# Last token group: indirect stores of units 5 to 8 on GpSimd behind four added waits on TensorE semaphores

## The reference

```python
xn = _layernorm(x)
# L1 attention: r, k, v are products with xn; a cumulative sum over time; a norm per batch; a product with Wo
r = sigmoid(xn @ Wr.T); k = xn @ Wk.T; v = xn @ Wv.T
state = cumsum(k * v / scale, axis=time) * scale
normed = groupnorm(r * state) * gn_weight + gn_bias
attn = normed @ Wo.T
# L1 mixture: the two best experts of each token, softmax weights
top_w, top_i = top_k(xn @ gate_w.T, 2)
ffn = sum over the two experts of softmax(top_w) * (xn @ expert_w[e] + expert_b[e])
x = x + attn + ffn
```

## Time and profile before

| | us |
|---|---|
| device time, median of 3 runs | 438.25 (437.61 to 438.61) |
| device time of the profiled execution | 437.0 |
| its span in the profile | 435.3 |
| PE busy in the span | 418.9 |
| DVE busy | 345.7 |
| ACT busy | 183.6 |
| POOL busy | 170.7 |
| chain that ended last: share of PE, DVE, issue, POOL | 78%, 11%, 3%, 2% |

### The profile page before, as it was taken

How to read it: one execution, slowest core, us unless ns; L and a number is a source line. 1 busy time by engine, 2 the same in 40 slices (tenths; PEclk the granted TensorE clock), 3 DMA queues, 4 the chain that set the end, 5 groups by cost and what they waited for, 6 DMA issues and landing times.

```text
span 435.3 us, 7440 instructions
## 1 busy us (share of the span) xinstructions
PE 418.9 (96%) x2488; PEld 364.5 (84%) x2488; DVE 345.7 (79%) x1087; ACT 183.6 (42%) x361; POOL 170.7 (39%) x200
## 2 busy tenths in 40 slices
PE   7999999999999999999999999999999999889992
PEld 5788888978898989788899898788999898779882
DVE  6799998898997677989968788899795757268781
ACT  4745654442364456332734343336352342423130
POOL 1556469621054104310447325103420445606456
PEclk9999999999999999999999999999999999999997
DMA  8992899950011310000112200000107545302289
GB/s 278 399 321 81 232 268 271 271 149 2 0 58 40 98 49 2 0 1 2 49 49 69 78 2 1 2 0 31 68 2 203 186 121 164 105 12 75 75 215 279
DMA packets 30373, 46.87 MB, mean 108 GB/s; under 512 B 2696, under 2 KB 24480, under 8 KB 29824
## 3 DMA queue, kind: packets, MB, share of 16 engines
q1 hardware_dynamic: 25984, 35.75, 27.5%
q0 software_dynamic: 3360, 9.85, 7.8%
q10 hardware_dynamic: 992, 0.81, 0.6%
HBM read 22.74 MB, written 23.65 MB: 107 GB/s over the span
## 4 chain that ended last, share of the span: by engine, by line
PE 78%; DVE 11%; issue 3%; POOL 2%; another core or an unknown queue 2%; ACT 2%; DMA 1%; POOLq 0%; DVEq 0%; ACTq 0%
PE D L707 23%; PE G L707 21%; PE U L707 20%; PE M L707 7%; PE D L738 1%; DVE mid_lo L1366 1%; DVE mid L1489 1%; DVE rows L1503 1%; POOL sums_gate L656 1%; DVE carry_gain L1727 1%; PE M L857 1%; DMA rows<-x 1%; PE M L832 1%; DVE gamma L1729 1%
## 5 line engine op out<-in xcount | busy, mean ns | idle before, releaser
L707 PE MATMUL D<-w_hi,mid_hi 128*128 128x256 f32 x260 | 74.1, 285 | 0.1
L707 PE MATMUL D<-w_hi,mid_lo 128*128 128x256 f32 x260 | 73.6, 283 | 0.0
L707 PE MATMUL D<-w_lo,mid_hi 128*128 128x256 f32 x260 | 73.5, 283 | 0.0
L1108 ACT ACTIVATE mid<-G 128x512 f32<-128x512 f32 x64 | 37.8, 594 | 72.3 <-PE G L707 46.4
L1489 DVE TENSOR_TENSOR mid<-mid,U 128x512 f32<-128x512 f32 x64 | 42.7, 683 | 21.8 <-ACT mid L1108 10.5
L551 POOL TENSOR_TENSOR w_lo<-w_raw,w_hi 128x512 fp32r<-128x512 f32 x35 | 50.3, 1469 | 22.9 <-ACT w_hi L1077 12.1
L1503 DVE SCALAR_TENSOR_TENSOR rows<-D,weight,rows 128x256 f32<-128x256 f32 x128 | 54.0, 476 | 6.4 <-PE D L707 3.9
L1077 ACT ACTIVATE mid_hi<-mid 128x512 fp32r<-128x512 f32 x64 | 39.8, 631 | 38.6 <-DVE mid L1489 37.0
L1366 DVE TENSOR_TENSOR mid_lo<-mid,mid_hi 128x512 fp32r<-128x512 f32 x64 | 49.7, 797 | 4.8 <-ACT mid_hi L1077 3.3
L707 PEld LDWEIGHTS D<-w_hi,mid_hi 128*128 128x128 f32 x260 | 49.8, 191 | 1.8 <-issue 1.1
L707 PE MATMUL G<-xT_hi,w_hi 128*128 128x512 f32 x126 | 50.4, 400 | 0.3 <-POOL w_lo L551 0.3
(11 more groups left out here) (369 smaller groups left out, 956.0 us busy)
## 6 DMA issues: line engine op xcount, KB each, us to landing
sorted_rows<-weighted SPq DMA_DIRECT2D x8, 1542.0 KB, 20.1
stage<-sorted_rows SPq DMA_DIRECT2D x31, 128.5 KB, 2.1
w_raw<-weights SPq DMA_DIRECT2D x2, 1280.0 KB, 14.3
w_raw<-weights SPq DMA_DIRECT2D x2, 1024.0 KB, 22.9
rows<-x SPq DMA_DIRECT2D x7, 256.0 KB, 3.0
w_raw<-weights SPq DMA_DIRECT2D x2, 768.0 KB, 8.8
part<-rows SPq DMA_DIRECT2D x12, 128.0 KB, 2.3
sums_gate<-part SPq DMA_DIRECT2D x3, 512.0 KB, 7.2
```

The source lines that it names most:

```text
L707: ins = nc.tensor.matmul(out_ap, a, b, start=(first and n == 0), stop=(last and n == 3 * len(pairs) - 1))
L1108: nc.scalar.activation(mid[:, c, :], GU[2 * c][:, :], ACT.Silu).then_inc(silu_ready, 1)
```

## The change

In the last part of POOL's program, `return_rows(u)` gets one more wait for u = 5, 6, 7 and 8, after the two that it has and ahead of the unit's two indirect DMAs:

```diff
@@ -640,6 +640,10 @@
                 tiles = UNIT_TILES[u]
                 pool.wait_ge(to_row_made, u + 1)
                 pool.wait_ge(unit_evicted, u + 1)
+                if u == 5:
+                    pool.wait_ge(unit_ps, 8)
+                elif u in (6, 7, 8):
+                    pool.wait_ge(rkv_ps, at(LAST, 6, 2 * (u - 6) + 1))
                 for i, n in enumerate(tiles):
                     nc.gpsimd.indirect_dma_start(returned[:, :], bass.IndirectOffsetOnAxis(to_row[:, n:n + 1], 0),
                                                  made[u][:, i, :], None).then_inc(made_stored, 16)
```

## The result

| | before | after |
|---|---|---|
| median of the runs beside each other (us) | 437.93 (437.08 to 438.61, 4 runs) | 433.13 (432.57 to 433.61, 4 runs) |
| the profiled execution (us) | 437.0 | 432.89 |
| its span (us) | 435.3 | 431.2 |

The ratio is 0.9887, 95% interval 0.9871 to 0.9903: faster by 1.1%, or 4.8 us, where 3.0 were forecast. Here and in the experiments, ratios and ranges leave out two disturbed executions, one of the kernel before at 687 us and one of the last experiment's kernel at 1259 us.

The account below looks back on a forecast made before the run. PE, 78% of the chain, was taken as held by late increments under POOL's scatters. Gains 0.8 + 1.4 + 0.6 + 0.6 = 3.4 us, taken as 3.0, made 437.0 into 434.0, plus 1.25: 435.3 (8 in 10: 432.9 to 438.3).

Parts of the forecast that it names:

- The reading of the lag: At 379 to 383 us: TensorE's increments are handed on late, 2.5 to 5.4 us, while POOL has been scattering for a while.
- Step 1: Router in the last group: the logits' copy runs at 375.9, so PE's transpose L744 doesn't wait; 0.81 us.
- Step 2: PE behind that transpose: r of half 1, due at 381.5, no longer starts at 382.87; 1.4 us.
- Step 3: DVE's chain from `den_e` starts earlier, so unit 9's product on PE no longer waits until 388.26; 0.6 us.
- Step 4: PE's idle of 0.52 us ahead of unit 10's product, the same DVE queue one step later, goes; 0.6 us.
- 2.8 to 3.4 of shift for the last scatter: POOL's last scatter, at 412.71, on which the kernel's end hangs, comes 2.8 to 3.4 us earlier; taken as 3.0.
- More: Rival, chance 0.10: later scatters shift so that a delay among units 10 to 12 goes; 2 us more, 433.3.
- The four waits cost nothing.: POOL's waits for units 5 to 8 are free while unit 9's eviction is later than unit 8's pair.
- Partly: Rival, chance 0.17: a pair after a pause of 0.8 to 1.6 us still delays something; gain 0.8 to 1.8, 437.0.
- Slower: Rival, chance 0.12: any pair's second scatter delays, and pairs now lie over critical PE results; 1.2 us lost, 439.5.
- No change: Rival, chance 0.11: the stop at 379 to 383 us has another cause, or the tail's DMAs set the end; 438.2.
- Code loading: Possible other cause of the stop, within a rival of chance 0.11: one instruction block moved between 370 and 383 us.

Follow-up runs that it names:

- the last experiment's kernel: The changed kernel with one wait more, unit 4's pair also waiting for unit 7's product: median 431.71 us, ratio 0.9910 to the kernel before.
- the short fill: Kernel before with one GpSimd fill of 128x256 ahead of each pair of units 5 to 8, no waits: 436.55 us, ratio 0.9970.
- the first kernel with unit 4's put apart: Against the change, unit 4's pair waits too (unit 7's product) and units 5 to 8 wait one product later: 433.93 us, ratio 0.9917 to before.
- The long pause: Kernel before with three GpSimd fills of 128x512 ahead of each pair of units 5 to 8, no waits: 429.69 us, ratio 0.9996.

## Why the prediction was right, by its own steps

- **The reading of the lag.** `den_e`, `r_half` and the logits' copy were held by TensorE's late increments, and these by the run of scatters. Shown: moving the run moved the hold (to 386 to 404 us), splitting it in two left 2.1 us of PE's stops where another sitting's trace of before has 3.8, and with four pairs and unit 4's put apart as well none was left. That it is TensorE's increments and not every engine's, one hand-over inside the run shows: ACT's copy of the logits ends at 379.52 and PE, waiting for it, starts at 379.57. What the prediction did not see is the condition: on two other chips twelve scatters in a row hold nothing back. The trace of before could not tell this.
- **Step 1, the logits' copy, 0.8.** It starts at 376.21 (forecast 375.9), and PE reaches its transpose at 378.89 instead of 379.57: 0.7. (The trace of after runs 0.26 us late before the change begins, 356.88 against 356.62 for unit 1's first scatter, so each lead here is 0.26 too small.)
- **Step 2, 1.4.** r of half 1 starts at 380.79 instead of 382.87: 2.1 ahead, 1.4 more.
- **Step 3, 0.6.** Unit 9's product starts at 385.54 instead of 388.26: 2.7 ahead, 0.6 more.
- **Step 4, 0.6.** Unit 10's starts at 387.41 (forecast 387.4) instead of 390.91: 3.5 ahead, 0.8 more.
- **The last scatter, where the sum was too small.** The term "2.8 to 3.4 of shift for the last scatter", taken as 3.0, measured 4.0. From unit 9's first scatter to the last POOL took 21.36 us before (391.35 to 412.71) and takes 20.07 after (388.61 to 408.68): units 9 to 15 take 1.3 us less (18.71 on the second chip, where nothing is late). One late copy accounts for as much: unit 13's product came out 1.9 us late before (402.37, then 404.30) and 0.7 after (398.86, then 399.51). The prediction had named this as what it could place to 1.5 us at best. Which of them lose less can't be read in advance from the trace of before. SP's fetch of the returned rows (L514) waits for the same landings as the join, which the part on the kernel before leaves out; so the end hangs on the last scatter by both ways.
- **The rest of the difference, 0.7.** The profiled execution gained 4.1 us (437.0 to 432.9) and the medians 4.8: the one of before lay 0.9 below its median, the one of after 0.2 below.
- **The size.** The sum followed the right path and was too small (3.0 for 4.8 us): 433.13 us lies below the forecast's own range (433.7 to 436.3) and just inside the wide one (from 432.9). The nearest number is that of "More" (433.3), and the kind of thing it named, a delay among the later units that goes, did happen, at unit 13 and not at units 10 to 12.
- **"The four waits cost nothing."** On the second chip, where no gain hides them, the ratio is 0.9994 (0.9984 to 1.0003), with the last scatter 0.9 us later in the trace.
- **The rivals.** "Partly": a pause of 0.73 us ahead of unit 7's pair was enough, but 0.61 was not, neither between the pairs of the short fill nor ahead of unit 8's pair in the first kernel with unit 4's put apart. The pause alone doesn't decide: in the changed kernel's own tail a pair comes 0.89 us behind a run of four (400.87), and unit 15's transposes, done at 400.47, are copied out at 402.49. "Slower": the four pairs of the change held nothing up, but its mechanism is real: a run laid over critical products cost 4.5 us. "No change" is what every kernel tried on the other two chips showed, for a reason that the prediction did not have. Code loading, its other cause, doesn't fit: one block of instructions moves between 372 and 375 us in the traces of before and of after alike, and PE stands still from 379 to 383 only in that of before; and in the kernel with the moved run no block moves between 390 and 402 us, while ACT waits for unit 11's product.
- **The pages.** The rule quoted ahead is that increments follow one another at about 26 ns (the Trainium skill, "TensorE: Matmul & The Clock Gate", "The cost: per-tile semaphore tail"). The 0.04 us at 376.97 on the second chip agree with it. On the third chip so does `den_e` at 379.64, ahead of the moved run; unit 11's product, which waited for over 11 us under that run, doesn't.

**What stays open** is why the same program has the lateness on one chip and not on two others (each of the two had one sitting, so chip and sitting can't be told apart there), and why its cost on the third was 437.9 us in one sitting and 435.6 and 435.7 in two later ones. Which element holds an increment back isn't in the traces either; in the kernel with the moved run PE too stood still for 0.80 us ahead of a matmul at 401.72 for which the profile names no releaser. The long pause was run only where there was nothing to gain, and the waits of units 5 to 8 were not compared with those of 6 to 8 alone in one sitting with the lateness.

## What to carry to other kernels

When several engines stand still together although TensorE's results are done, compare each instruction's start with the end of the matmul that it waits for, and look at what GpSimd issues meanwhile. Runs of indirect DMAs are cheaply cut into pairs by waits on later products of TensorE; where they did no good here they did no measurable harm, with slack in the queue behind them. A run moved whole onto critical products cost more than it saved. Run the kernel before again on another chip before the mechanism is taken for a property of the program.

## What the runs showed of the hardware that was not expected

- The same program took 429.9 and 430.0 us on two chips and 435.6 to 437.9 on a third. What the traces show of the difference is the late hand-over of TensorE's increments to other engines while GpSimd issues indirect DMAs in close succession.
- On that third chip one increment was taken over 11 us late, under twelve scatters in a row, and only 2 us after the last of them.
- Idling of 2.16 us under this hold was followed by a granted clock of 0.50 for 3 us, which made a product of twelve matmuls last 2.70 us instead of 1.52.
